# A gated delta-rule mixer in four stacked layers on one core: the norms of queries and keys summed by a half selector in four column strips

## The reference

```
q = l2norm(silu(causal_conv(x @ w_q)))    # 16 heads of 64
k = l2norm(silu(causal_conv(x @ w_k)))    # 16 heads of 64
v = silu(causal_conv(x @ w_v))            # 16 heads of 128
l2norm(x) = x * rsqrt(sum(x * x, -1) + 1e-6)
per token: S = S * exp(g);  S += outer(k, (v - k.S) * beta);  o = (q / 8).S
out = rms_norm(o) * norm_w * silu(x @ w_g) @ w_out
```

## Time and profile before

| | |
|---|---|
| median of 3 runs | 5253.84 us (5246.8 to 5258.72) |
| profiled execution | 5220.28 us, its span 5218.5 us |
| mean granted clock of TensorE | 0.925 |
| busy shares of the span | PE 89%, PEld 62%, DVE 74%, ACT 51%, POOL 46% |
| first chunk to last chunk of this mixer | 114 to about 2464 us |

### The profile page before, as it was taken

The page is one execution under the profiler, slowest core; times in us unless marked ns, Lnnn a source line. Parts: engine busy times, 40 slices in busy tenths (PEclk is TensorE's granted clock), DMA queues, the critical chain, the costliest instruction groups (busy, mean ns, idle before and its releaser), DMA issues. The chain is left out here.

```text
span 5218.5 us, 111235 instructions
## 1 busy us (share of the span) xinstructions
PE 4631.6 (89%) x40474; PEld 3241.2 (62%) x40474; DVE 3837.1 (74%) x9047; ACT 2679.9 (51%) x6583; POOL 2375.8 (46%) x1924
## 2 busy tenths in 40 slices
PE   5999999999999999998899899954688779988998
PEld 3776777677777777776666466521365655655665
DVE  5777867777777777785786588456899458856874
ACT  2554554555554555454786488344100218856882
POOL 2544544555445444453674377134222127734751
PEclk6999999999999999999899899876799569999998
DMA  2000000000000000001000000000000000000000
GB/s 88 8 9 10 9 7 10 10 7 8 9 10 10 8 8 10 10 10 36 1 0 26 5 0 0 7 0 0 9 1 1 1 31 1 0 26 5 0 0 17
DMA packets 170111, 52.95 MB, mean 10 GB/s; under 512 B 142304, under 2 KB 166112, under 8 KB 168928
## 3 DMA queue, kind: packets, MB, share of 16 engines
q1 hardware_dynamic: 168160, 44.24, 3.8%
q10 hardware_dynamic: 1536, 3.21, 0.2%
HBM read 36.92 MB, written 10.49 MB: 9 GB/s over the span
## 5 line engine op out<-in xcount | busy, mean ns | idle before, releaser
L864 DVE SCALAR_TENSOR_TENSOR gd_qkT<-gd_ps,gd_w_qk,gd_qkT 128x256 f32<-128x256 f32 x768 | 364.7, 482 | 152.5 <-ACT gd_qkT L686 131.9
L430 PE MATMUL gd_ps<-gd_taps,gd_xwins 128*128 128x512 f32 x1024 | 464.6, 596 | 0.0
L1642 ACT ACTIVATE L_ffn_s<-L_ffn_s,L_ffn_nb,L_ffn_r 128x128 f32<-128x128 f32 x1024 | 419.5, 482 | 3.1
L1462 POOL TENSOR_TENSOR L_ffn_t<-L_ffn_t 128x512 f32<-128x512 f32 x128 | 190.2, 1486 | 398.7 <-DVE L_ffn_t L1683 398.7
L430 PEld LDWEIGHTS gd_ps<-gd_taps,gd_xwins 128*128 128x128 f32 x1024 | 192.4, 191 | 190.8 <-issue 185.2
L1080 POOL TENSOR_TENSOR gd_gV<-gd_g,cst 128x512 f32<-128x512 f32 x128 | 130.3, 1039 | 275.3 <-PE gd_ps L547 275.3
L1681 DVE TENSOR_TENSOR L_ffn_t<-L_ffn_ps,L_ffn_sb_rope 128x512 f32<-128x512 f32 x256 | 176.9, 691 | 101.0 <-PE L_ffn_ps L1487 101.0
L1530 PEld LDWEIGHTS L_ffn_ps<-L_ffn_kT,L_ffn_qT 64*64 64x64 f32 (+1 forms) x4096 | 149.5, 137 | 114.2 <-issue 98.8
L1119 POOL TENSOR_TENSOR gd_gV<-gd_Tc,cst 128x1024 f32<-128x1024 f32 x32 | 60.6, 1892 | 340.7 <-DVE gd_Tc L939 340.7
L1464 POOL TENSOR_TENSOR L_ffn_r<-L_ffn_ss,L_ffn_mhalf 128x8 f32<-128x8 f32 x128 | 210.9, 1647 | 10.5 <-DVE L_ffn_ss L1705 5.2
L1471 POOL TENSOR_TENSOR L_ffn_r<-L_ffn_ss,L_ffn_mhalf 128x8 f32<-128x8 f32 x128 | 210.9, 1648 | 0.0
(11 more groups left out here) (396 smaller groups left out, 13993.3 us busy)
## 6 DMA issues: line engine op xcount, KB each, us to landing
L_ffn_sb_rope<-in_rope SPq DMA_DIRECT2D x4, 2048.0 KB, 8.3
gd_tap_row<-in_L_attn_conv_v SPq DMA_DIRECT2D x2, 2048.0 KB, 15.9
gd_blocks<-gd_nA SPq DMA_DIRECT2D x256, 16.0 KB, 1.7
gd_Z<-gd_blocks SPq DMA_DIRECT2D x32, 128.0 KB, 2.0
gd_inverses<-gd_Z SPq DMA_DIRECT2D x32, 128.0 KB, 1.7
gd_Tc<-gd_inverses SPq DMA_DIRECT2D x256, 16.0 KB, 1.9
L_ffn_sb_wqkv<-in_L_ffn_wqkv SPq DMA_DIRECT2D x4, 768.0 KB, 9.1
out<-out_tok SPq DMA_DIRECT2D x8, 256.0 KB, 2.7
```

The lines of the kernel that those rows point to most:

```text
L430: ins = pe.matmul(ps[4 + i % 2][:], xwin(j)[:, t:t + P], taps[:, t, 512 * i:512 * (i + 1)], start=(t == 0), stop=(t == TAPS - 1))
L864: ins = dve.scalar_tensor_tensor(produced(j, i), ps[6 + i % 2][:, P + t:P + t + WIDE], w_tap[:, at, t:t + 1], produced(j, i), ALU.mult, AL ...
L1462: pool.tensor_tensor(t1[b][:, K], t1[b][:, K], t2[b][:, K], ALU.add).then_inc(la.k_sum.sem, 1)
L1642: ins = act.activation(s[b][:, i, k], s[b][:, i, k], ACT.Exp, scale=r[b][:, h:h + 1], bias=nb[b][:, i, k:k + 1])
```

## The change

The roles are swapped: the selector, widened to 32 columns (30 of them zero), becomes the weights, and the squares stream. Four matmuls of 128x512 each write a strip of 32 partitions of bank 6; strip q takes tiles q and q+4, so that all eight tiles lie in 512 columns, head-major in partitions and tokens in columns. ScalarE copies the bank to the first 512 columns of `delta` (`copy_sums`), and TensorE turns it back to token order with four transposes (`turn_sums`). VectorE reads two columns of every 32 and writes them with two instructions, one for each half of the heads.

The order changes with it: the sums stand behind all four gates, the turning behind the state products, ScalarE's copy behind the silu of the last gate. The prologue has sums, copy and turning in one row.

```diff
@@ -27,7 +27,7 @@
 C_HEADS = C_HEAD + 16
 C_EYE = C_HEADS + P
 C_HALVES = C_EYE + BASE * BASE
-C_END = C_HALVES + 2
+C_END = C_HALVES + 32
 
 
 def constant_table():
@@ -269,6 +269,7 @@
         PT, yT, y, squares = decay, X, delta, X
         Xc = X[:, 0:H // 2]
         Zc = Z[:].rearrange("p h x -> p (h x)")[:, 0:2 * 8 * 32].rearrange("p (r k x) -> p r k x", r=2, k=H // 2)
+        qk_sums = delta[:].rearrange("p h x -> p (h x)")[:, 0:4 * P]
         qk_sq = delta[:].rearrange("p h x -> p (h x)").rearrange("p (i t) -> p i t", i=PAIRS)
         NB = P // BASE
         blocks_dram = nc.dram_tensor("gd_blocks", (NB, H, BASE, BASE), F32, kind="Internal").ap()
@@ -290,7 +291,7 @@
         abs_s = sig("abs", 1)
         c_mm, c_s, nec_s = sig("sums_mm", 1), sig("sums_exp", 1), sig("neg_ec", 1)
         qk_mm, tap0_s, conv_s, silu_s = sig("qk_mm", PAIRS), sig("first_tap", PAIRS), sig("convolved", PAIRS), sig("qk_silu", PAIRS)
-        sq_s, ss_mm, ss_s, inv_k_s, nrm_s = sig("squares", 4), sig("square_sums_mm", 1), sig("square_sums", 1), sig("k_inverse", 1), sig("k_norms", 1)
+        sq_s, sum_mm, sum_out, ss_mm, ss_s, inv_k_s, nrm_s = sig("squares", 4), sig("norm_sums_mm", 1), sig("norm_sums_out", 1), sig("square_sums_mm", 1), sig("square_sums", 2), sig("k_inverse", 1), sig("k_norms", 1)
         v_mm, v_out, vn_s = sig("v_mm", 4), sig("v_out", 4), sig("v_scaled", 4)
         gate_mm, gate_out = sig("gate_mm", 4), sig("gate_out", 4)
         tk_mm, tk_out = sig("k_turned", 2), sig("k_token_major", 2)
@@ -315,7 +316,6 @@
         out_mm, out_s = sig("out_mm", 1), sig("x1", 1, primed=True)
         chain_d, chain_i, chain_c = sems("gd_chain_decays"), sems("gd_chain_inverse"), sems("gd_chain_conv")
         PROD = slice(P, P + XWIN)
-        SUMS = slice(448, 480)
         SCORES = slice(32, 64)
         LAST = B * NC - 1
 
@@ -410,14 +410,17 @@
                     pe.matmul(ps[6 + i % 2][:, PROD], w_pair[:, PAIRS * (j % 2) + i], xflat[:, bass.ds(b * (PAD + T) + c * P, XWIN)],
                               start=True, stop=True).then_inc(qk_mm.sem, 1)
 
-                def square_sums(turn, q):
-                    w(sq_s.now(turn, q))
-                    for i in (2 * q, 2 * q + 1):
-                        for c in range(2):
-                            at = SUMS.start + 2 * PAIRS * c + 2 * i
-                            ins = pe.matmul(ps[6][:, at:at + 2], qk_sq[:, i, P * c:P * (c + 1)], cst[:, C_HALVES:C_HALVES + 2], start=True, stop=True)
-                    if q == 3:
-                        ins.then_inc(ss_mm.sem, 1)
+                def square_sums(turn):
+                    w(sq_s.now(turn))
+                    for q in range(4):
+                        ins = pe.matmul(ps[6][32 * q:32 * (q + 1)], cst[:, C_HALVES:C_HALVES + 32], qk_sq[:, q:PAIRS:4], start=True, stop=True)
+                    ins.then_inc(sum_mm.sem, 1)
+
+                def turn_sums(turn):
+                    w(sum_out.now(turn))
+                    for k in range(4):
+                        ins = pe.transpose(ps[6][:, P * k:P * (k + 1)], qk_sums[:, P * k:P * (k + 1)], ident)
+                    ins.then_inc(ss_mm.sem, 1)
 
                 def project_ab(n, j):
                     w(win.now(n))
@@ -620,10 +623,12 @@
                 def body(n, b, c, j, s, follows, more):
                     turn_k(n, j)
                     for i in range(4):
-                        if follows:
-                            square_sums(n + 1, i)
                         project_gate(n, j, i)
+                    if follows:
+                        square_sums(n + 1)
                     state_products(n, j)
+                    if follows:
+                        turn_sums(n + 1)
                     query_products(n, j)
                     solve(n)
                     if follows:
@@ -660,8 +665,8 @@
                 for i in range(PAIRS):
                     produce(0, 0, i, 0, 0)
                 w(conv_s.now(0))
-                for i in range(4):
-                    square_sums(0, i)
+                square_sums(0)
+                turn_sums(0)
                 w(ss_s.now(0))
                 project_ab(1, 1)
                 for i in range(4):
@@ -705,6 +710,10 @@
                     for q in range(2):
                         w(tk_mm.now(n, q))
                         act.activation(k_tok[:, 4 * q:4 * q + 4].rearrange("p i x -> p (i x)"), ps[4 + q][:], ACT.Copy).then_inc(tk_out.sem, 1)
+
+                def copy_sums(turn):
+                    w(sum_mm.now(turn))
+                    act.activation(qk_sums, ps[6][:], ACT.Copy).then_inc(sum_out.sem, 1)
 
                 def total_exps(n):
                     w(c_mm.now(n))
@@ -760,6 +769,8 @@
                     token_major_k(n)
                     for i in range(4):
                         silu_gate(n, i)
+                    if follows:
+                        copy_sums(n + 1)
                     late(n)
                     if follows:
                         total_exps(n + 1)
@@ -799,6 +810,7 @@
                     if i:
                         silu(0, -2, i - 1)
                 silu(0, -2, PAIRS - 1)
+                copy_sums(0)
                 exp_ab(1)
                 for i in range(4):
                     silu_v(0, i)
@@ -871,14 +883,16 @@
 
                 def square_sums(turn, j, s):
                     w(ss_mm.now(turn))
-                    sums = ps[6][:, SUMS].rearrange("p (c k two) -> p c two k", two=2, k=4)
-                    by_head = lambda t: t[:].rearrange("p c h -> p (c h)").rearrange("p (c two k) -> p c two k", two=2, k=4)
+                    sums = ps[6][:].rearrange("p (a c k x) -> p a c x k", a=2, c=2, x=32)[:, :, :, 0:2]
+                    by_head = lambda t: t[:].rearrange("p c (a two k) -> p a c two k", a=2, two=2)
+                    for a in range(2):
+                        if j % 2 == 0:
+                            dve.tensor_scalar(by_head(k_ss)[:, a], sums[:, a], 1e-6, None, ALU.add).then_inc(ss_s.sem, 1)
+                        else:
+                            dve.tensor_scalar(by_head(q_eps)[:, a], sums[:, a], 1e-6, DK * EPS, ALU.add, ALU.mult).then_inc(ss_s.sem, 1)
                     if j % 2 == 0:
-                        dve.tensor_scalar(by_head(k_ss), sums, 1e-6, None, ALU.add).then_inc(ss_s.sem, 1)
                         w(ss_s.now(turn))
                         dve.reciprocal(k_inv[:], k_ss[:]).then_inc(inv_k_s.sem, 1)
-                    else:
-                        dve.tensor_scalar(by_head(q_eps), sums, 1e-6, DK * EPS, ALU.add, ALU.mult).then_inc(ss_s.sem, 1)
 
                 def key_scores(n):
                     w(beta_s.now(n))
```

## The result

The changed kernel takes 5333.73 us (median of 4 runs, 5296.88 to 5380.28) against 5250.32 us before (median of 4, 5238.31 to 5258.72). The ratio is 1.0137, 95% interval 1.008 to 1.0195; it is one of means and leaves out the slowest run, 5380.28, which is over 1.5% above the fastest (5321.44 / 5249.42). It is slower, where 21 us less were forecast, and 5333.73 lies outside the range of 5213 to 5266. The profiled execution took 5337.35 us, its span is 5335.6 us.

A forecast was written before the change was run, and what follows sets the result against it. TensorE's order sets the pace, but the chunk front runs against an unchanged inverse-block DMA. Gains of 5.3, 2.2, 0.55, 3.2, 6.8 and 3 us make 21, taken off the 5253.84 median: 5233 us, range 5213 to 5266.

The forecast's parts named there:

- the strips: TensorE, behind the gates: eight passes on four column strips run four at once, 0.95 us; 1.75 and 3.44 kept as ends.
- rivals 1 and 4: Strips run two at a time, 1.75 us, kernel 5242 (14%); or one after another, 3.44 us, kernel 5283 (8%).
- Gate wait: TensorE, first gate behind the key transposes: waits for ScalarE's first copy, 0.4 us that the sums used to hide.
- query products: TensorE, ahead of the solve: would start at 8.15 us after the chunk's start instead of 9.86.
- Residues: VectorE, behind the turned sums: would run from 8.55 to 12.8 us, against 9.22 to 13.45 before.
- the direct gain per chunk: Solve's start moves up to the blocks' arrival: 1.05 us in five chunks, 0.44 in five, 3.2 over two others.
- the 1.5 taken: Inverse blocks were taken to arrive 1.5 us after SP's last load issue, read as 1.49 in one chunk.
- the signs of being wrong: Listed: strip starts in pairs or single, mask waiting for residues, SP's issues moved, more 0.50 windows, new loop-end stalls.
- the prologue: Before the chunks: 6.99 us of sums at half clock become less, gaining 3 us.
- the two half-clock chunks: Chunks with an issue stall in the key transposes stay at half clock; 3.4 us gained each, 6.8 together.
- rival 3: Longer waits bring more half-clock stretches, about 10 us each: 5253 with two added, 5273 with four; 15%.
- 0 for the chunks that the DMA holds: The other 15 chunks with a successor, held by the inverse-block DMA or nearly, were to gain 0.

The follow-up runs named there:

- early2: Changed kernel with second half of query products computed three times, strips directly behind key transposes, turning behind gates; 5218.57 us, ratio 0.9957 to the kernel before.
- fill2: Changed kernel with the second half of the query products computed three times in every chunk; 5222.34 us, ratio 0.9971 to the kernel before.
- cut: Kernel before, with the 16 matmuls of the sums cut to one from chunk 1 on, no strips, old order; 5401.74 us, ratio 1.033.
- late: Kernel before, with three spare DMA transfers issued by SP ahead of the eight inverse-block loads; 5526.3 us, ratio 1.0566.
- early0: Changed kernel with strips behind the key transposes and turning behind the gates, query products computed once; 5386.18 us, ratio 1.0282 to the kernel before.
- fill1: Changed kernel with the second half of the query products computed twice in every chunk; 5245.56 us, ratio 1.0005 to the kernel before.
- order: Kernel before, with the four quarters of the sums moved behind the four gates, nothing else; 5277.26 us, ratio 1.0066.

## Why the prediction was wrong

**Right in mechanism and size: the strips.** Four at once, 1.00 us against 0.95 taken; rivals 1 and 4 (two at a time, one after another) did not happen: the eight passes begin in two groups of four, each within 20 ns, 0.45 us apart. The Trainium skill's figure for four row tiles ("TensorE: Matmul & The Clock Gate", Part 3, measured speedup: 3.07) would give 1.12; this trace has 8 x 0.43 / 1.00 = 3.4 times, for column strips with fp32 passes, and the measurement decides.

**Nearly right: the front.** Gate wait 0.25 against 0.4. Query products at 8.64 against 8.15: state products, turning and query products start 0.2, 0.35 and 0.5 us later than my steps had them. Residues 0.35 late, with nobody waiting for them here (L515 at 11.80). The tiling of the array (full width, strips, half height) changes three times more per chunk than before, not twice, and no idle time stands ahead of any of these changes in the chunk at 2150.20.

**Too large: the direct gain per chunk.** The time from the last issue to L515 is 1.35 us in this chunk, as the 1.5 taken. But the chain ahead of it was longer. SP's timeline after, and the corresponding first issue of before:

```profile
2154.37 0.34 SPq L387 DMA_DIRECT2D gd_inverses<-gd_Z  x1
2156.90 3.75 SPq L391 DMA_DIRECT2D gd_Tc<-gd_inverses  x8
```

```profile
2050.11 0.34 SPq L387 DMA_DIRECT2D gd_inverses<-gd_Z  x1
```

The store of the inverses leaves 4.17 us after the chunk's start in both, and the eight loads begin 2.53 us behind it, where 51.83 - 50.11 = 1.72 us was the distance in the 2045.94 chunk. So L515 came 0.44 us earlier than before and not 1.1. It is one of the signs of being wrong that I had named, SP's issues moved against the key transposes. Why the store took longer was not tried. In the prologue the strips waited for GpSimd's last squares, where the quarters had begun with the first:

```profile
68.22 1.94 PE L416 MATMUL gd_ps<-gd_delta,cst 128*32 128x512 f32 x8 [3.78 <-POOL gd_delta L1083]
72.41 0.63 PE L427 MATMUL gd_ps<-gd_w_ab,gd_xwins 128*128 128x32 f32 x2 [0.43 <-DVE gd_k_ss L890]
```

and before, the same work behind the sums:

```profile
73.98 0.64 PE L424 MATMUL gd_ps<-gd_w_ab,gd_xwins 128*128 128x32 f32 x2 [0.36 <-DVE gd_k_ss L877]
```

It starts at 72.41 where it was 73.98, 1.6 us earlier and not 3, and nothing of it reached the chunks: the first one starts at 114.14, before at 114.10.

**Too small: the loop's ends.** I took the two half-clock chunks as staying at half clock, with 3.4 us each to gain. They returned to full clock (above) and gave 21 us together. No step of the forecast has that: it is luck, in the change's favour.

**Near the forecast by coincidence: early2 and fill2.** early2 gains 0.43% of 5237, 22 us, and fill2 0.29%, 15 us, against the 21 forecast, but not by the steps of the forecast. Its 24 chunks that keep the full clock in both traces are together 9 us longer in early2 than before, since the filling puts the solve later (13.55 us after the start of the chunk at 2042.46, against 12.24 in the one at 2045.94), and two chunks more have a long half-clock stretch that before had a short one or none. What is shorter are the two chunks behind the loop's ends, together 144.98 us where they took 165.16:

```profile
430.76:503.25 72.49, 70.23 (x746) 51.90 (x747) 55.21 (x152) 39.29 (x112) 33.62 (x31) 1.00 0.06 10
```

In fill2 they take 150.92. The traces do not account for the gain in full: the mixer takes 2354 us in early2's and 2350 in the one of before, whose execution took 5220.28 us where the 29 runs beside early2 have a median of 5236.59.

**The step that failed** is rival 3, "More half-clock stretches", and what I let it rest on. I saw that the saved time turns into a longer wait ahead of the solve ("the wait for the arrival grows from 0.4 to 1.9 us to as much as 2.5") and counted it as nothing gained, not as something lost: the sum has 0 for the chunks that the DMA holds. I took "the wait of 1.87 at 1108.87 lies in a stretch whose mean is 0.99" as evidence that such waits are harmless, although the forecast's own went up to 2.5 us and a stall of 2.51 us stood beside a fall in the earlier trace rows. I gave the rival 15%, and priced two to four stretches of 10 us. There were 13 long ones, and the chunks with them took 156 us more than before. One costs 85.70 - 71.71 = 14 us, because the clock falls at the head of the solve and comes back late: behind the first chunk, 8 of the 12 stretches last into the full-width products behind the solve, 4 end within it after 17 to 24 us. What stood ahead of the wait in the row of before was an unbroken front: key transposes, sums and gates in turn without a gap. The removed passes had been doing a second job. That the longer wait does it is shown from both sides: less work (cut), a later arrival alone (late) and the wait in one piece (early0) each bring the half-clock time; filling alone takes more than half of it away (fill1) or nearly all (fill2).

**Which chunk falls** is sorted in part by the wait ahead of the solve, counted behind the first chunk. In early0, with few and small gaps in the front, the 15 chunks with the longest waits (2.25 to 3.84 us) had a long fall there and the 16 others (up to 2.20 us) did not. Before, waits of 1.87, 1.93 and 1.97 us passed without a fall. In the changed kernel, which has gaps of 0.25 us and more in its front, a long fall followed 9 of 11 waits of 1.84 us or more, 3 of 10 waits of 1.18 to 1.50 us, and none of the 10 shorter. But in late, without gaps, one long fall followed a wait of 1.54 us while waits of 2.36 to 2.82 us passed without one. So longer waits are followed by a fall more often, and that is all that these traces sort; that the small gaps add to it is possible and not shown, since no run adds them alone.

**Left open.** Why waits of 1.36 to 1.50 us were followed by a fall in some chunks and not in others; what passes of two columns do to the clock beside idle time; why the stalls at the loop's ends are gone with the strips; and why the loads begin 2.5 us or more behind the store of the inverses in nine of the changed kernel's chunks, and about 1.75 us in most others.

## What to carry to other kernels

Before taking work off an engine whose clock depends on its activity, ask what it will do in the freed time; if the answer is to wait for a DMA that does not move, the gain is nothing and the loss can be a half-clock stretch through the next stage. Add up the idle time and the time at half clock of both traces before reading single chunks. Price such a stretch by the stage behind it, not by the gap. Where the wait can't be shortened, repeating a product whose result is already there is a cheap test of that reason, and may be the better kernel (0.9971 for fill2 against 1.0137). And where a total comes out as forecast, look whether its parts do: early2's 22 us were not the 21 of the forecast.

## What the runs showed of the hardware

Four 128x32 column strips of fp32 passes, each streaming 512 columns from all 128 partitions, run at once: eight passes in 1.00 us. The granted clock fell with TensorE fully busy, behind 3.6 us of two-column passes (order). And once down it stayed at 0.50 through more than 25 us of unbroken work, most of it 64x64 passes, and returned among the 128x128 products (the chunk at 1139.03); in four other chunks it returned earlier, after 17 to 24 us.
